# The job of the second layer's norms, moved one step later in the repeated part of a two-layer kernel

## The chip, the cores and the metric

The kernel runs on one core of one Trainium2 chip. The metric is device time in microseconds (us) of one execution. The kernel before takes 874.63 us (median of three runs, 871.47 to 875.64). Engines are called by the profile's names: PE (matrix products), DVE (vector), ACT (activations), POOL, and SP, which only issues transfers.

## The reference, cut to what matters

Two transformer layers work on x of shape (8, 512, 128): eight sequences of 512 tokens, width 128, 16 heads.

```
xn = layernorm(x)
x  = x + attention0(xn) + ffn0(xn)     # differential attention: two maps of 16 heads with 4 numbers each
xn = layernorm(x)
x  = x + attention1(xn) + ffn1(xn)     # rotated q and k, one map of 16 heads with 8 numbers each
```

Each attention is softmax(scale * q k^T) v per head. The feed-forward part of the second layer is three products (128 to 512 to 512 to 128) with weights of +1 and -1, and a relu after the first and the second.

The softmax is computed with a fixed shift in place of the row's maximum. That is allowed where a bound on the scores holds: for the second layer, the product of the largest norm of a q row and of a k row. The norms are what this case is about: two small products add up the squares of q and of k per head, and a chain of small vector operations makes a flag of them. If the flag says that the bound fails, an exact maximum is computed instead, and that branch is not taken with these inputs.

## The kernel before, in words

**Units and steps.** The attention work is 24 units in a fixed order. A(b) and B(b) are the two maps of the first layer for sequence b, C(b) is the second layer. A unit has 16 steps. In each step PE makes the scores of four heads against 128 keys (`scores`, L845, four products of 128x512 into the pairs of banks `ps_s`), ACT takes the exponential of them in two instructions (L707, two banks each), and PE multiplies the probabilities of the step before the last with the values (`pv`, L863, four products that add into one bank, `ps_pv`). So step s of a unit has on PE: scores(s), pv(s-2), and then the jobs of the step.

**Jobs.** Everything else (projections, feed-forward, norms, rotations) is put into steps by tables written out by hand: FIRST, LOOP and LAST (L75, L103, L120). LOOP holds one body of three units, A(b), B(b), C(b-1), and is written out for b = 2, 3, 4, 5. PE, DVE and ACT each walk the same table, and each runs its own part of every entry in the order of the table; each engine's queue runs in order. POOL and SP have no part in the entries spoken of here.

**One bank for all jobs.** The products of all jobs go to a single bank, `ps_misc`. Before a job's first product PE waits until the job before it has been read out of that bank (`PLAN.before`, L743). Who reads is in TAKER (L60): DVE for v1 and qk_norm1, ACT for ff0.

**The jobs around the change**, all in unit A(b), for sequence b-1 of the second layer:

- v1 (step 9): 32 products of 128x128 (L728), then DVE copies the bank to the values (L1167).
- take (step 9): no product. DVE waits for pv of step 7 and transposes `ps_pv` into `pv_sb` (L1308). PE's pv of step 8, the first of the next pair of head groups, waits for it (L869), as it starts anew in that bank.
- qk_norm1: two bf16 products of 32x512 (L779), then DVE reduces the bank to one number a row (L1170), which frees the bank, and six small operations make the flag (L1172 to L1183).
- ff0 with block 3 (step 10): two products (L732, L733), then ACT's relu (L657) into `ff_out`, and DVE splits that in two parts (L1104, L1106).
- project1 (step 11): 32 products (L728), DVE adds them to x.
- exact1 (step 12): PE and DVE read the flag (L813, L1242), and DVE sets the shift.

```
                if PLAN.before[item] is not None:
                    e, n = PLAN.before[item]
                    pe.wait_ge(TAKEN[e], n)
...
                pe.wait_ge(exps_made, 2 * S + 2)
                if s % 8 == 0:
                    wait(pe, pv_taken, 2 * U.u + s // 8)
```

Of the kernel before, what the change touches and what calls it, by code (L numbers as in the profile page):

```python
# [60 lines left out]
             qk_norm1="dve", w_t="dve", quant_t="dve", quant_mm="dve",  # L61
# [41 lines left out]
LOOP = [  # L103
    {0: [("ff0", -1, 0)], 1: [("take", -2, "C", 1), ("ff0", -1, 1)], 2: [("regroup", -2, "C", 1)], 3: [("q1", -1)],
     4: [("rope", -1, "q", 0), ("ff0", -1, 2)], 5: [("out_t1", -2), ("rope", -1, "q", 1)], 6: [("k1", -1)],
     7: [("rope", -1, "k", 0), ("rope", -1, "k", 1)], 9: [("v1", -1), ("take", 0, "A", 0), ("qk_norm1", -1)], 10: [("ff0", -1, 3)],
     11: [("regroup", 0, "A", 0), ("project1", -2)], 12: [("exact1", -1)], 13: [("ff1", -1, 0), ("ff1_b", -1, 0), ("norm0", 1, 0)],
     14: [("ff1", -1, 1), ("norm0", 1, 1)], 15: [("ff1_b", -1, 1), ("norm0", 1, 2)]},
    {0: [("ff1", -1, 2), ("norm0", 1, 3)], 1: [("take", 0, "A", 1), ("norm0", 1, 4), ("ff1_b", -1, 2)],
# [1371 lines left out]
```

## Time and profile before

| | us |
|---|---|
| median of three runs | 874.63 |
| the profiled execution | 872.51 |
| its span, first to last instruction | 870.7 |
| PE busy | 808.3 (93%) |
| ACT busy | 765.2 (88%) |
| DVE busy | 545.4 (63%) |
| POOL busy | 36.0 (4%) |

The span leaves 1.8 us of the execution's own time around it. PE and ACT pass work back and forth in every step. The profile's mean of PE's granted clock over the span is 0.98 of full speed. Busy shares are means over units of different kinds; the stretch of the change lies in the A units, and the rows below are of that stretch.

### The profile page before, as it was taken

What the parts mean: (1) busy time and instruction counts of PE and PEld (TensorE: products, weight loads), DVE (VectorE), ACT (ScalarE), POOL (GpSimd) and SP (SyncE); (2) the same over time, 40 slices, a digit from 0 to 9 for tenths busy, and PEclk for the clock granted to TensorE, in tenths of its full rate; (3) what the DMA queues carried; (4) which work ended last, traced back from release to release, by engine and by line L of the source; (5) the groups of instructions that cost most, each with busy time, mean ns of one, the idle gap of its engine ahead of it and who ended that gap; (6) DMA issues with size and microseconds to landing.
All of it is one profiled execution on the core that took longest, in us unless ns stands there. A gap on an engine that the chain in (4) does not pass through costs nothing.

```text
span 870.7 us, 17841 instructions
## 1 busy us (share of the span) xinstructions
PE 808.3 (93%) x6767; PEld 287.7 (33%) x6767; DVE 545.4 (63%) x1205; ACT 765.2 (88%) x856; POOL 36.0 (4%) x57
## 2 busy tenths in 40 slices
PE   6688898999999989999999999999998999999995
PEld 4122222342333323333233323333242323333342
DVE  6667478676774666746775567756677476476321
ACT  3679997889889998999889998999988999889984
POOL 5000000000000000000000000000000000000000
PEclk9889998999999999999999999999999999999998
DMA  6807315630728015460527407281164704205100
GB/s 182 170 9 149 52 50 148 146 49 8 209 49 142 11 69 142 104 99 1 148 62 142 59 1 209 50 138 16 49 162 100 102 17 133 52 1 167 43 13 13
DMA packets 41618, 75.52 MB, mean 87 GB/s; under 512 B 5872, under 2 KB 7024, under 8 KB 41520
## 3 DMA queue, kind: packets, MB, share of 16 engines
q1 hardware_dynamic: 39612, 68.45, 36.1%
q0 software_dynamic: 1824, 5.70, 2.1%
q8 instruction: 57, 0.93, 0.5%
q14 instruction: 33, 0.27, 0.1%
q10 hardware_dynamic: 92, 0.16, 0.1%
HBM read 36.84 MB, written 35.65 MB: 83 GB/s over the span
## 4 chain that ended last, share of the span: by engine, by line
PE 72%; ACT 11%; DVE 9%; issue 5%; DMA 1%; DVEq 0%; SPq 0%; ACTq 0%; POOL 0%; POOLq 0%
PE ps_pv L877 31%; PE ps_s L858 20%; ACT probs L707 11%; PE ps_misc L728 7%; PE ps_misc L732 7%; PE ps_misc L733 5%; PE ps_misc L721 2%; DMA q_ab<-shift 1%; DVE pv_sb L1308 1%; DVE v_aug L1167 1%; DVE tmp L1159 0%; DVE h_lo L1106 0%; DVE tmp L1158 0%; PE ps_misc L779 0%; ACT ff_out L657 0%
## 5 line engine op out<-in xcount | busy, mean ns | idle before, releaser
L707 ACT ACTIVATE probs<-ps_s 128x1024 f32<-128x1024 f32 x768 | 726.5, 1046 | 61.8 <-PE ps_s L858 60.5
L877 PE MATMUL ps_pv<-probs,v_aug 128*32 128x512 f32 x3072 | 413.5, 610 | 10.2 <-ACT probs L707 5.8
L858 PE MATMUL ps_s<-q_ab,k_ab 18*128 18x512 f32 (+1 forms) x1088 | 143.5, 500 | 28.8 <-ACT probs L707 20.3
L858 PEld LDWEIGHTS ps_s<-q_ab,k_ab 18*128 18x128 f32 (+1 forms) x1088 | 54.7, 184 | 197.7 <-ACT probs L707 153.7
L877 PEld LDWEIGHTS ps_pv<-probs,v_aug 128*32 128x32 f32 x3072 | 61.9, 108 | 118.5 <-issue 81.2
L732 PE MATMUL ps_misc<-h_hi,k_w 128*128 128x512 f32 x192 | 85.7, 446 | 2.7 <-DVE v_aug L1167 1.2
L858 PE MATMUL ps_s<-q_c,k_c 34*128 34x512 f32 x448 | 84.8, 453 | 0.0
L1104 DVE CAST h_hi<-ff_out 128x512 fp32r<-128x512 f32 x64 | 27.4, 428 | 89.0 <-ACT ff_out L657 87.5
L1308 DVE STREAM_TRANSPOSE pv_sb<-ps_pv 128x512 f32<-128x512 f32 x48 | 34.4, 717 | 70.8 <-PE ps_pv L877 67.5
L733 PE MATMUL ps_misc<-h_lo,k_w 128*128 128x512 f32 x192 | 75.9, 395 | 0.0
L732 PEld LDWEIGHTS ps_misc<-h_hi,k_w 128*128 128x128 f32 x192 | 35.9, 187 | 88.4 <-issue 48.8
L858 PEld LDWEIGHTS ps_s<-q_c,k_c 34*128 34x128 f32 x448 | 36.1, 184 | 74.7 <-ACT probs L707 60.2
L657 ACT ACTIVATE ff_out<-ps_misc 128x512 f32<-128x512 f32 x64 | 39.1, 610 | 17.9 <-PE ps_misc L733 13.8
L1106 DVE TENSOR_TENSOR h_lo<-ff_out,h_hi 128x512 fp32r<-128x512 f32 x64 | 44.3, 692 | 2.2
L733 PEld LDWEIGHTS ps_misc<-h_lo,k_w 128*128 128x128 f32 x192 | 36.1, 188 | 4.3
L1191 DVE TENSOR_TENSOR x_all<-ps_misc,x_all 128x512 f32<-128x512 f32 x24 | 16.6, 692 | 26.3 <-PE ps_misc L721 12.8
L728 PE MATMUL ps_misc<-xn_t,w_qk 128*32 128x512 f32 x248 | 32.3, 592 | 0.0
L1167 DVE COPY v_aug<-ps_misc 128x512 f32<-128x512 f32 x14 | 9.7, 692 | 27.5 <-PE ps_misc L728 27.1
L615 POOL CAST h_hi<-xn_t 128x512 fp32r<-128x512 f32 x8 | 4.9, 608 | 502.9 <-DVE xn_t L1135 502.9
L1320 DVE TENSOR_TENSOR heads<-pv_sb,recip 128x256 f32<-128x256 f32 x48 | 20.4, 425 | 1.7
L728 PE MATMUL ps_misc<-wp,quant_t 128*32 128x128 f32 x512 | 17.8, 282 | 2.7 <-DVE quant_t L1327 2.7
L728 PEld LDWEIGHTS ps_misc<-wp,quant_t 128*32 128x32 f32 x512 | 15.2, 113 | 12.8 <-issue 11.3
(164 smaller groups left out, 563.1 us busy)
## 6 DMA issues: line engine op xcount, KB each, us to landing
parts_dram<-qk_parts SPq DMA_DIRECT2D x32, 512.0 KB, 3.7
parts_dram<-qk_parts SPq DMA_DIRECT2D x62, 256.0 KB, 4.1
q_ab<-parts_dram SPq DMA_DIRECT2D x60, 128.0 KB, 4.6
k_ab<-parts_dram SPq DMA_DIRECT2D x60, 128.0 KB, 5.9
q_c<-parts_dram SPq DMA_DIRECT2D x14, 512.0 KB, 7.5
k_c<-parts_dram SPq DMA_DIRECT2D x14, 512.0 KB, 8.8
out_dram<-x_all POOLq DMA_DIRECT2D x8, 256.0 KB, 6.8
x_all<-in_L_attn_x_dram POOLq DMA_DIRECT2D x7, 256.0 KB, 6.1
```

The lines of the kernel that those rows point to most:

```text
L657: nc.scalar.activation(ff_out[:], ps_misc[:], ACT.Relu).then_inc(job_taken_act, 1)
L707: nc.scalar.activation(probs[:, U.slot(s), 2 * half:2 * half + 2], ps_s[:, 2 * pair:2 * pair + 2], ACT.Exp, scale=SCALE[U.layer]).then_inc ...
L728: ins = nc.tensor.matmul(ps[c, :], w[:, c], x, start=True, stop=True)
L732: nc.tensor.matmul(ps, w, hi, start=start, stop=False)
L733: return nc.tensor.matmul(ps, w, lo, start=False, stop=stop)
L858: ins = nc.tensor.matmul(ps_s[:, bank, :], k[row:row + n, slot, c * P:(c + 1) * P], q[row:row + n, slot, :], start=True, stop=True)
L877: ins = nc.tensor.matmul(ps_pv[32 * j:32 * j + 32, :], v_aug[:, U.v, c, a:a + 32], probs[:, U.slot(s), j, :], start=c == 0 and not odd, st ...
L1104: nc.vector.tensor_copy(hi, ff_out[:]).then_inc(ff_split, 1)
L1106: nc.vector.tensor_tensor(lo, ff_out[:], hi.bitcast(F32), ALU.subtract).then_inc(ff_split, 1)
L1167: taken(nc.vector.tensor_copy(own_values(unit("C" if layer else "A", b).v), ps.rearrange("p (t h e) -> p t h e", t=T, h=H)))
L1308: nc.vector.transpose(pv_sb[:], ps_pv[:]).then_inc(pv_taken, 1)
L1320: nc.vector.tensor_tensor(dst, v[:, :, :, 0:HD], rows(recip[:], HD), ALU.mult).then_inc(regroup_ops, 1)
```

## The change

In LOOP, the entry of qk_norm1 moves from the end of step 9 of unit A to the head of step 10, in front of the ff0 entry. Nothing else is changed: the order of the jobs in the bank `ps_misc` and the order of DVE's and ACT's work stay the same.

```diff
-     7: [("rope", -1, "k", 0), ("rope", -1, "k", 1)], 9: [("v1", -1), ("take", 0, "A", 0), ("qk_norm1", -1)], 10: [("ff0", -1, 3)],
+     7: [("rope", -1, "k", 0), ("rope", -1, "k", 1)], 9: [("v1", -1), ("take", 0, "A", 0)], 10: [("qk_norm1", -1), ("ff0", -1, 3)],
```

On PE the order was scores(9), pv(7), v1, qk_norm1, scores(10), pv(8), ff0. It is now scores(9), pv(7), v1, scores(10), pv(8), qk_norm1, ff0. FIRST and LAST, which have qk_norm1 for the sequences 0, 5, 6 and 7, are as before.

## Rows read from the trace of the kernel before

**Rows 1.** The page: busy time by engine, and the chain that ended last
```profile
PE 808.3 (93%) x6767; PEld 287.7 (33%) x6767; DVE 545.4 (63%) x1205; ACT 765.2 (88%) x856; POOL 36.0 (4%) x57
PE 72%; ACT 11%; DVE 9%; issue 5%; DMA 1%; DVEq 0%; SPq 0%; ACTq 0%; POOL 0%; POOLq 0%
```
**Rows 2.** Chain of waits in the second body: start, length, what
```profile
325.89 0.70 DVE v_aug L1167
327.03 0.44 PE ps_s L858 x4
```
**Rows 3.** Timeline of PE, same stretch: start, length, what, [idle before, releaser]
```profile
324.76 1.06 PE L728 MATMUL ps_misc<-w_v,xn_t 128*32 128x128 f32 x32
326.64 0.39 PE L779 MATMUL ps_misc<-qk_sq,head_sel 128*32 128x512 bf16 x2 [0.81 <-DVE v_aug L1167]
326.96 0.51 PE L858 MATMUL ps_s<-q_ab,k_ab 18*128 18x512 f32 x4
327.55 1.06 PE L877 MATMUL ps_pv<-probs,v_aug 128*32 128x512 f32 x8
328.55 0.50 PE L732 MATMUL ps_misc<-h_hi,k_w 128*128 128x512 f32 x1
```
**Rows 4.** Timeline of DVE, same stretch
```profile
325.89 0.69 DVE L1167 COPY v_aug<-ps_misc 128x512 f32<-128x512 f32 x1 [0.79 <-PE ps_misc L728]
326.69 0.72 DVE L1308 STREAM_TRANSPOSE pv_sb<-ps_pv 128x512 f32<-128x512 f32 x1
327.51 0.68 DVE L1170 TENSOR_REDUCE norm_max<-ps_misc 64x1 f32<-64x512 f32 x1
329.20 0.14 DVE L1183 CAST flags<-flag_f 1x1 int32<-1x1 f32 x1
```
**Rows 5.** Timeline of ACT, same stretch
```profile
327.56 1.94 ACT L707 ACTIVATE probs<-ps_s 128x1024 f32<-128x1024 f32 x2 [1.41 <-PE ps_s L858]
```
**Rows 6.** Timeline of PE, first and last of the four bodies
```profile
224.36 0.39 PE L779 MATMUL ps_misc<-qk_sq,head_sel 128*32 128x512 bf16 x2 [0.81 <-DVE v_aug L1167]
531.03 0.39 PE L779 MATMUL ps_misc<-qk_sq,head_sel 128*32 128x512 bf16 x2 [0.81 <-DVE v_aug L1167]
```
**Rows 7.** Timeline of PE and DVE behind the loop, jobs in steps of their own
```profile
633.30 1.06 PE L728 MATMUL ps_misc<-w_v,xn_t 128*32 128x128 f32 x32
634.29 0.50 PE L858 MATMUL ps_s<-q_ab,k_ab 18*128 18x512 f32 x4
795.14 1.06 PE L877 MATMUL ps_pv<-probs,v_aug 128*32 128x512 f32 x8
796.02 0.39 PE L779 MATMUL ps_misc<-qk_sq,head_sel 128*32 128x512 bf16 x2
796.45 0.68 DVE L1170 TENSOR_REDUCE norm_max<-ps_misc 64x1 f32<-64x512 f32 x1 [0.16 <-PE ps_misc L779]
```
**Rows 8.** Timeline of DVE and PE ahead of the loop, PE waiting for the reduction
```profile
133.96 0.68 DVE L1170 TENSOR_REDUCE norm_max<-ps_misc 64x1 f32<-64x512 f32 x1
134.69 1.08 PE L728 MATMUL ps_misc<-w_v,xn_t 128*32 128x128 f32 x32
```
**Rows 9.** Timeline of PE around two falls of its clock
```profile
140.05 0.50 PE L732 MATMUL ps_misc<-h_hi,k_w 128*128 128x512 f32 x1 [1.16 <-DVE v_aug L1167]
141.47 0.50 PE L732 MATMUL ps_misc<-h_hi,k_w 128*128 128x512 f32 x1 [0.69 <-ACT ff_out L657]
671.19 1.77 PE L877 MATMUL ps_pv<-probs,v_aug 128*32 128x512 f32 x8 [1.93 <-DVE pv_sb L1308]
676.06 0.51 PE L858 MATMUL ps_s<-q_ab,k_ab 18*128 18x512 f32 x4
```
**Rows 10.** Busy time by stretch; the number behind POOL's is PE's granted clock
```profile
140.00:150.00 10.00, 9.03 (x44) 2.77 (x48) 6.99 (x21) 5.62 (x8) 0.00 (x0) 0.66 0.60 126
670.00:680.00 10.00, 8.64 (x84) 2.96 (x84) 4.04 (x8) 6.65 (x8) 0.00 (x0) 0.83 0.97 187
320.00:330.00 10.00, 8.60 (x95) 3.03 (x96) 7.90 (x18) 8.40 (x11) 0.00 (x0) 1.00 0.74 247
```

## The prediction

> **What bounds the kernel now.** I read four views, in this order. The page first: PE is busy for 93% of the span and ACT for 88%, and the chain that ended last lies on PE for 72% and on DVE for only 9% [rows 1]. So a wait matters where it holds PE up; DVE's own load does not. Second, the chain of waits in the stretch of the change, for the question whether the moved job is on it. It is: DVE's copy of v stands in the chain with 0.70 us, and the norm products and the scores behind it are fed from it [rows 2]. Third, the timelines of PE, DVE and ACT side by side. On PE the reader is to see one gap of 0.81 us, in front of the norm products, while DVE copies v out of the shared bank [rows 3]; on ACT a gap of 1.41 us, as the scores of step 10 stand behind those products [rows 5]. The same gap of 0.81 us stands in each of the four bodies of the loop, of which the first and the last are shown [rows 6]. That is what the change removes. Fourth, the stretches with PE's granted clock, for what gaps have done to it.
>
> **What goes.** PE no longer waits for the copy of v before step 10. Where v and the next scores follow without a job between them, the scores start 634.29 - 633.30 = 0.99 us after the second part of v's products [rows 7]. Here that is 324.76 + 0.99 = 325.75, against 326.96 before [rows 3]: 1.21 us earlier. They last 0.51 us, to 326.26.
>
> **What is late next.** Behind these scores stands pv(8), and it waits for something else: for DVE's transposition of the same bank (take). DVE does that behind the copy of v. The copy can't start earlier than now, since v's products don't; it runs from 325.89 for 0.69, and the transposition from 326.69 for 0.72, so to 327.41 [rows 4]. PE's pv(8) starts at 327.55, 0.14 later [rows 3], and 0.59 behind its scores where the chain gives scores 0.44 [rows 2]. So it is the transposition that already sets pv(8) before the change, and pv(8) stays at 327.55. All of the 1.21 us is given back there, as a gap of 327.55 - 326.26 = 1.29 us on PE.
>
> **What is added.** Now the norm products stand behind pv(8), and ff0 behind them in the same bank, with the reduction by DVE between the two. Step by step, from pv(8)'s start:
>
> - pv to norm products: 796.02 - 795.14 = 0.88 us [rows 7], so 328.43.
> - norm products to reduction: 796.45 - 796.02 = 0.43, with DVE idle before it [rows 7], so 328.86. Here DVE is free from 327.41.
> - the reduction: 0.68 [rows 7], so to 329.54.
> - its end to PE's next product: 134.69 - (133.96 + 0.68) = 0.05 [rows 8], so ff0 starts at 329.59.
>
> Before the change ff0 started at 328.55 [rows 3], since the reduction (327.51 to 328.19 [rows 4]) was hidden behind scores and pv of step 10. That cover is gone, and with it PE gains a second gap, from the end of the norm products, 328.43 + 0.39 = 328.82, to 329.59: 0.77 us. Loss: 329.59 - 328.55 = 1.04 us in each body.
>
> Queued behind ff0 are on PE the scores of step 11, and on ACT its relu, with the exponentials of step 11 behind that. ACT gets the scores of step 10 some 1.2 us earlier but then stands before the relu, so its head start doesn't last. All of PE, ACT and DVE go on 1.04 us later. I find nothing with a fixed time that would take this up: DMA has 1% of the chain [rows 1]. The six small operations behind the reduction end 329.34 - 328.19 = 1.15 us after it [rows 4], so at 330.69; the flag's reader is two steps on, behind ff0, a step's scores and pv and 32 products of project1, which alone take more than that. No transfer is moved, no POOL or SP instruction either. Sum of the waits: 4 x 1.04 = 4.2 us.
>
> **What the gaps do to the clock.** The trace has two places where PE's clock fell from 2.4 to 1.2 GHz within work like this. At 140.05 and 141.47 PE had gaps of 1.16 and 0.69 us, 1.85 in all between 138.89 and 141.47; at 671.19 it had one of 1.93 [rows 9]. In the first stretch the granted clock averages 0.66 over 10 us, which is 0.34 x 10 / 0.5 = 6.8 us at the lower level; in the second 0.83, so 3.4 us [rows 10]. The single gap of 0.81 of now left it at 1.00 [rows 10]. The change makes gaps of 1.29 and 0.77 us, 2.06 in all, from 326.26 to 329.59. That looks like the rows where the clock fell, not like the one where it held; but the two gaps stand further apart than those, so I don't expect it each time. Price of one fall: from 671.19 to 676.06 PE did pv, scores, pv and v in 4.87 us [rows 9]. At full speed these are 1.00 [rows 3], 0.44 [rows 2], 0.88 and 0.99 [rows 7], in sum 3.31. So 1.6 us for the shorter fall; for the longer I take twice that, 3.1. The bounds over four bodies are 0 and 4 x 3.1 = 12.4 us; I take one fall of the short kind in the four, 1.6, as the nearest row is a single gap of nearly this sum and the two gaps here are spread more.
>
> The Trainium skill's page "TensorE: Matmul & The Clock Gate", section "Why this matters for your kernels", says that the clock drops mid-kernel for one idle gap far longer than either of these. By that rule no body would meet a fall, and the sum would be the waits alone. The trace does not agree with it: at 140 no single gap was over 1.16 us, and the clock fell all the same [rows 9, 10].
>
> **Sum.** 4.2 + 1.6 = 5.8 us. The profiled execution took 872.51 (span 870.7 and 1.8 around it), so it would take 878.3. It lies 2.1 under the median of the runs, 874.63; the median is what a set of new runs is compared with, so I predict 874.63 + 5.8 = 880.4 us.
>
> **Rivals.**
>
> 1. *The waits alone, the clock holds.* For it: the gap of 0.81 did nothing to the clock, and the new gaps are separated by 1.3 us of products. Against it: the pair at 140. Time: 874.63 + 4.2 = 878.8.
> 2. *The clock falls in three or four bodies.* For it: 2.06 us of gaps are more than either row. Time: 4.2 + 3 x 1.6 = 9.0, so 883.6; with the longer kind up to 4.2 + 4 x 3.1 = 16.6, 891.
> 3. *Faster: pv(8) doesn't wait for the transposition.* Place: PE's wait in step 10. If it passed at once, pv(8) would start at 325.75 + 0.44 = 326.19, the norm products at 327.07, the reduction at 327.51 (the transposition ends at 327.41, so DVE is just free), and ff0 at 327.51 + 0.68 + 0.05 = 328.24 against 328.55: 0.31 us gained in each body, 1.2 in all, 873.4. It decides by whether pv(8) starts before 328.55 - 2.04 = 326.51, as the four steps above take 2.04 us from there to ff0. Against it: pv(8) follows the transposition's end by 0.14 now.
> 4. *Taken up later.* The 1.04 us of a body could vanish in slack downstream: 874.6. For it speaks only that the chain has 5% "issue" time that the profile doesn't explain [rows 1].
>
> **How the numbers follow.** A difference of about 0.5% (4.4 us) is what a measurement here can tell from none. Chances: the forecast (waits and one or two falls) 0.42; rival 1, 0.30; rival 2, 0.16; rival 3, 0.05; rival 4, 0.07. Forecast and rival 2 lie over 4.4 us. Rival 1 lies at 4.2, just inside, so I split it, 0.12 over and 0.18 within. Rivals 3 and 4 are within, except for 0.03 which I leave for a gain of over 0.5% that no row shows. So slower 0.70, same 0.27, faster 0.03. The range leaves out rival 3 and the far half of rival 2: 876.0 to 886.0; its lower end holds rival 1 in a set of runs as fast as the profiled one (872.51 + 4.2 = 876.7).
>
> **What would show it.** In the changed kernel's timeline of PE: scores of step 10 right behind v, in each of four bodies; a gap of about 1.3 us before pv(8), released by DVE's transposition of ps_pv; norm products 0.88 behind that pv; a gap of about 0.8 us before ff0, released by the reduction. On ACT: the exponentials of step 10 some 1.2 us earlier, and a gap of about 2 us before the relu. The distance from v's products to ff0 grows by 1.04 us. Stretches of the granted clock around the four bodies show whether it fell, and how often. The prediction is wrong if pv(8) starts earlier after v than now, if ff0 keeps its distance to v, or if the bodies (now (531.03 - 224.36) / 3 = 102.2 us apart [rows 6]) don't grow by 1 us or more.

## The result, and the profile after

The changed kernel is slower. In a first set of seven runs its median is 883.44 us (877.44 to 884.08) against 872.83 for the kernel before; the ratio is 1.0102, with a 95% interval of 1.0072 to 1.0132, so 8.9 us by the ratio (10.6 between the two medians). In a second set on another occasion (experiment after_again) it is 878.08 against 872.49, ratio 1.0071, 1.0046 to 1.0097, so 6.2 us. The forecast was 5.8 us: 4.2 of waits and 1.6 of one fall of PE's clock. The waits came out within 0.02 us a body. What comes on top of them is more than the 1.6 (4.7 and 2.0 us by the two ratios) and varies from one execution to the next; part of it is the clock.

The profiled execution took 877.44 us, the shortest of the first set. Its span, from the page:

```profile
span 875.6 us, 17841 instructions
PE 807.9 (92%) x6767; PEld 287.8 (33%) x6767; DVE 545.4 (62%) x1205; ACT 765.5 (87%) x856; POOL 36.0 (4%) x57
```

The busy times are those of before [rows 1] within 0.4 us, so the 4.9 us that the span has grown is no added work. The timeline of PE in the second body (start, length, what, idle before and who ended it), to be read against [rows 3]:

```profile
326.81 1.06 PE L728 MATMUL ps_misc<-w_v,xn_t 128*32 128x128 f32 x32
327.79 0.51 PE L858 MATMUL ps_s<-q_ab,k_ab 18*128 18x512 f32 x4
329.59 1.06 PE L877 MATMUL ps_pv<-probs,v_aug 128*32 128x512 f32 x8 [1.29 <-DVE pv_sb L1308]
330.45 0.41 PE L779 MATMUL ps_misc<-qk_sq,head_sel 128*32 128x512 bf16 x2
331.63 0.50 PE L732 MATMUL ps_misc<-h_hi,k_w 128*128 128x512 f32 x1 [0.78 <-DVE norm_max L1170]
```

The reader is to see two gaps where there was one of 0.81 us, each with the releaser that the prediction named. From v to ff0 it is now 331.63 - 326.81 = 4.82 us; before it was 328.55 - 324.76 = 3.79 [rows 3]. That is 1.03 us more. The timeline of DVE, against [rows 4]:

```profile
327.93 0.69 DVE L1167 COPY v_aug<-ps_misc 128x512 f32<-128x512 f32 x1 [0.78 <-PE ps_misc L728]
328.73 0.72 DVE L1308 STREAM_TRANSPOSE pv_sb<-ps_pv 128x512 f32<-128x512 f32 x1
330.90 0.68 DVE L1170 TENSOR_REDUCE norm_max<-ps_misc 64x1 f32<-64x512 f32 x1 [1.45 <-PE ps_misc L779]
```

DVE stands 1.45 us between its second and its third operation. Before, it had the norm products ready for it there. And of ACT, against [rows 5]:

```profile
328.40 1.94 ACT L707 ACTIVATE probs<-ps_s 128x1024 f32<-128x1024 f32 x2 [0.21 <-PE ps_s L858]
332.40 0.60 ACT L657 ACTIVATE ff_out<-ps_misc 128x512 f32<-128x512 f32 x1 [2.07 <-PE ps_misc L733]
```

ACT starts step 10's exponentials 1.59 us after the start of v's products instead of 2.80, and gives it back in front of the relu. The chain of waits has both of DVE's operations on it now:

```profile
327.93 0.70 DVE v_aug L1167
328.73 0.73 DVE pv_sb L1308
329.59 1.06 PE ps_pv L877 x8
330.90 0.69 DVE norm_max L1170
```

Last, the stretches by the four bodies; the number behind POOL's is PE's granted clock, 1.00 everywhere in the same four stretches before:

```profile
220.00:240.00 20.00, 17.42 (x168) 7.16 (x164) 11.37 (x25) 14.40 (x17) 0.61 (x1) 0.91 0.72 188
325.00:345.00 20.00, 17.42 (x176) 7.61 (x172) 12.83 (x28) 15.71 (x18) 0.58 (x1) 1.00 0.72 188
430.00:450.00 20.00, 17.49 (x173) 7.58 (x166) 12.02 (x27) 15.44 (x19) 0.56 (x1) 1.00 0.69 175
535.00:555.00 20.00, 17.96 (x148) 7.41 (x148) 12.71 (x35) 15.31 (x18) 0.56 (x1) 1.00 0.64 156
```

The clock fell once, in the first body: 0.09 x 20 / 0.5 = 3.6 us at 1.2 GHz. What that costs can be read from the distance between the reductions (L1170) of successive bodies, which start like this:

```profile
225.98 0.68 DVE L1170 TENSOR_REDUCE norm_max<-ps_misc 64x1 f32<-64x512 f32 x1 [1.45 <-PE ps_misc L779]
330.90 0.68 DVE L1170 TENSOR_REDUCE norm_max<-ps_misc 64x1 f32<-64x512 f32 x1 [1.45 <-PE ps_misc L779]
434.02 0.68 DVE L1170 TENSOR_REDUCE norm_max<-ps_misc 64x1 f32<-64x512 f32 x1 [1.45 <-PE ps_misc L779]
537.39 0.68 DVE L1170 TENSOR_REDUCE norm_max<-ps_misc 64x1 f32<-64x512 f32 x1 [1.45 <-PE ps_misc L779]
```

| | body 1 to 2 | 2 to 3 | 3 to 4 |
|---|---|---|---|
| before | 102.28 | 102.06 | 102.33 |
| after | 104.92 | 103.12 | 103.37 |
| difference | 2.64 | 1.06 | 1.04 |

The second and third differences are the waits alone; the first has the fall as well, 2.64 - 1.05 = 1.6 us. So this execution is the forecast nearly term by term: 4 x 1.04 + 1.6 = 5.8. From the last reduction ahead of the loop to the first one behind it the time grew from 502.11 to 507.71 us, by 5.6. The whole execution grew by 4.9 (877.44 - 872.51); the difference lies ahead of and behind the loop.

### The profile page after: what moved, and what is told of

It is laid out like the page before. It is cut to its first block, busy times and chain, and to the rows that moved or that the text cites. A ratio compares the mean times of both kernels' runs of the same rounds, so it can differ in the third digit from the quotient of the medians.

```text
span 875.6 us, 17841 instructions
## 1 busy us (share of the span) xinstructions
PE 807.9 (92%) x6767; PEld 287.8 (33%) x6767; DVE 545.4 (62%) x1205; ACT 765.5 (87%) x856; POOL 36.0 (4%) x57
## 4 chain that ended last, share of the span: by engine, by line
PE 71%; ACT 11%; DVE 10%; issue 5%; DMA 1%; DVEq 0%; SPq 0%; ACTq 0%; POOL 0%; POOLq 0%
PE ps_pv L877 31%; PE ps_s L858 19%; ACT probs L707 11%; PE ps_misc L728 7%; PE ps_misc L732 7%; PE ps_misc L733 5%; PE ps_misc L721 2%; DMA q_ab<-shift 1%; DVE pv_sb L1308 1%; DVE v_aug L1167 1%; DVE norm_max L1170 0%; DVE h_lo L1106 0%; ACT ff_out L657 0%; DVE tmp L1159 0%; DVE tmp L1089 0%
## 5 line engine op out<-in xcount | busy, mean ns | idle before, releaser
L1308 DVE STREAM_TRANSPOSE pv_sb<-ps_pv 128x512 f32<-128x512 f32 x48 | 34.4, 717 | 70.9 <-PE ps_pv L877 67.5
```

Source lines behind the costliest of these rows:

```text
L1308: nc.vector.transpose(pv_sb[:], ps_pv[:]).then_inc(pv_taken, 1)
```

## The experiments

**Fill the gaps.** If what exceeds 4.2 us is the clock, it must go when PE has something to do in the gaps, though the waits stay. Of the edits only the lines and entries that differ are shown; "..." marks what is left out between them.

```diff
+            def fill(S, n):
+
+                pe.wait_ge(exps_made, 2 * S)
+                for _ in range(n):
+                    nc.tensor.transpose(ps_s[:, 2 * ((2 * S + 2) % 3), 0:P], ident[:], ident[:])
...
                     scores(U, s)
+                    if U.kind == "A" and U.b in range(2, 6) and s == 10:
+                        fill(U.first_step + s, 7)
...
+                            if S % STEPS == 10:
+                                fill(S, 4)
```

> The changed kernel with both of PE's new gaps filled: in step 10 of the four bodies PE does 7 transposes of the identity after the scores and 4 after the norm products, into a bank of ps_s that is free there and is written anew by the next scores. The waits stay where they are, as the fill is about as long as the gaps (1.0 of 1.29 us and 0.6 of 0.77 us). Theory (the time over the 4.2 us of waits is lost to falls of PE's clock): the clock no longer falls in the bodies, and the time is 872.8 + 4.2 = 877.0, with runs close to each other (within 2 us beside those of the kernel before). Rival (the waits cost more than the trace shows, or something else is lost): the time stays at 881 to 884 as in the changed kernel.

Measured: 877.39 us against 874.04 before in the same set, ratio 1.0048 (1.0029 to 1.0067), 4.2 us. The timeline of PE in its first body:

```profile
227.65 0.98 PE L885 MATMUL ps_s<-ident 128*128 128x128 f32 x7
229.00 1.06 PE L877 MATMUL ps_pv<-probs,v_aug 128*32 128x512 f32 x8 [0.36 <-DVE pv_sb L1319]
230.20 0.66 PE L885 MATMUL ps_s<-ident 128*128 128x128 f32 x4
231.04 0.50 PE L732 MATMUL ps_misc<-h_hi,k_w 128*128 128x512 f32 x1 [0.19 <-DVE norm_max L1181]
```

The work starts where it did (229.00 - 227.20 = 1.80 us from scores to pv, as 329.59 - 327.79 = 1.80 above), and the granted clock is 1.00 in all four bodies. The time is that of the waits alone, within an interval of 2.5 to 5.9 us. That interval lies below that of the first set of the changed kernel (1.0072 to 1.0132) and overlaps with that of the second (1.0046 to 1.0097), so the timed runs alone don't settle what the fill gives back. One part of the expectation missed: the runs were not within 2 us of each other (876.18 to 882.66), so the bodies aren't the only place where executions differ. The profiled execution shows it: it took 880.70 us with no fall in the bodies, and it is 2.9 us behind the kernel before already at the last reduction ahead of the loop (136.87 against 133.96).

With only the second gap filled (the edit is against the one above):

```diff
-                        fill(U.first_step + s, 7)
+                        fill(U.first_step + s, 0)
```

> The changed kernel with only the second gap (before ff0, 0.77 us) filled, by 4 transposes of the identity; the gap of 1.29 us before pv of step 8 stays. Theory (it takes both gaps for the clock to fall, as single ones of 1.29 us in the spread version's profile were followed by no fall): 877 to 878, as with both filled. Rival (the gap of 1.29 us is enough by itself in some executions): 879 to 883, with falls in the bodies of the profile.

878.13 us against 872.49, ratio 1.0057 (1.0032 to 1.0082), 5.0 us. In its profile no body had a fall, though each had the gap of 1.29 us. That agrees with the theory that it takes both gaps, but one profile of four bodies can't exclude a rare fall. The time says nothing either way: the changed kernel with nothing filled took 878.08 us in the same set, so on those runs the fill gained nothing that can be measured.

**The same kernel again**, for more profiles of the changed kernel with their times.

> The changed kernel once more, unaltered, for a second profile beside its time. Its first profiled execution took 877.44 us with one fall of the clock in the four bodies, while most of its other runs took 882 to 884. Theory: those have two to four falls of some 1.6 us or more. So this profile, if it lies at 881 or more, shows at least two stretches at the lower level within the four bodies, and each body without one is 103.2 us from the next; if it lies under 879 it shows one at most. Rival (the waits themselves last longer in the slow executions): the gaps before pv of step 8 and before ff0 differ from 1.29 and 0.77 us, with no more falls.

> The changed kernel once more, one look, for a third profile beside its time. Expected as in the second: the time over 876.4 to 877 is 1.6 us or more for each fall of the clock in the four bodies, give or take the 1 to 2 us that the falls ahead of and behind the loop differ by between executions.

> The changed kernel once more, one look. The three profiles so far had one fall in the four bodies each, at 877.4 to 879.6 us; its slowest executions, at 883 to 884, were not seen yet. If this one takes over 881 us, the theory wants two falls or more in the bodies; if under 880, none or one.

> The changed kernel once more, one look, expected as the fourth: over 881 us two falls or more in the bodies, under 880 none or one.

| profile | time | falls in the bodies | distances of the bodies |
|---|---|---|---|
| first | 877.44 | body 1 | 104.92, 103.12, 103.37 |
| after_again | 877.47 | body 1 | 104.88, 103.09, 103.34 |
| after_look3 | 879.63 | body 3 | 103.40, 103.08, 104.92 |
| after_look4 | 879.55 | body 3 | 103.36, 103.08, 104.93 |
| after_look5 | 883.67 | bodies 1 and 4 | 104.88, 103.11, 103.36 |

The gaps are 1.28 to 1.29 and 0.78 us in all twenty bodies; so the waits are the same whatever an execution takes, and the rival falls. Six of the twenty bodies have a fall, and in all six it shows first behind the second gap: ff0's first product takes 0.58 to 0.80 us there instead of 0.50. The twenty are not independent draws. The three executions with a fall in body 1 have their last reduction ahead of the loop at 133.5 to 134.0 us; the two with one in body 3 have it at 135.8, and are alike to within 0.1 us at every reduction. That also accounts for most of their 879.6 us: they have one short fall, as the first profile has, and are 2.2 us behind it before the loop begins. The one of 883.67 us has two, as expected, the second of the long kind (a stretch and a line of PE in after_look5):

```profile
535.00:550.00 15.00, 12.81 (x100) 5.50 (x100) 6.32 (x16) 8.79 (x11) 0.56 (x1) 0.77 0.87 215
693.87 0.51 PE L858 MATMUL ps_s<-q_ab,k_ab 18*128 18x512 f32 x4 [3.35 <-DMA q_ab<-shift]
```

0.23 x 15 / 0.5 = 6.9 us at 1.2 GHz. From the fourth body's reduction to the next one, behind the loop, it is 106.65 us, against 103.83 in the first profile: 2.8 us for a long fall. But its span is 881.9 - 875.6 = 6.3 us over the first profile's, and 3.4 of these lie outside the bodies, between 644 and 739 (95.04 against 91.61 from one reduction to the next), around the second line above: a wait of 3.35 us for the transfer of the shift, where the first profile has 0.70.

**The tail.** In both kernels the clock as a rule falls around 671 to 677, behind a gap of 1.93 us [rows 9]. In after_look5 it didn't, and the long wait came in its place. To see whether the one makes the other, the kernel before had that gap filled:

```diff
+                    if (U.kind, U.b, s) == ("B", 6, 10):
+                        fill(U.first_step + s, 10)
```

> The kernel before (norm products in their old place), in which PE fills its gap of 1.93 us in step 10 of unit B(6), behind the loop, with 10 transposes of the identity (1.5 us) after the scores, into a bank of ps_s that is free there. In the kernel before that gap is followed by a fall of the clock, and PE then waits only 0.49 us for the transfer of the shift at the start of unit A(7). In the changed kernel's slow profile (883.67 us) the clock did not fall there, PE waited 3.35 us for that transfer instead, and the clock fell behind that wait, for 6.8 us. Theory (a tail of the time of both kernels comes from there): with the gap filled the clock doesn't fall at 671, PE waits 2 to 3.5 us for the transfer, the clock falls behind it, and the time is 2 to 3.5 us longer than the kernel before, 874.5 to 876. Rival (the transfer's lateness in the slow profile has another cause): no fall, the wait grows by at most 1.5 us, and the time is that of the kernel before or up to 1 us less.

876.27 us against 874.46, ratio 1.0031 (1.0013 to 1.0049): 2.7 us slower. PE, and the granted clock behind POOL's number:

```profile
670.83 1.31 PE L896 MATMUL ps_s<-ident 128*128 128x128 f32 x10 [0.41 <-ACT probs L707]
672.35 1.06 PE L877 MATMUL ps_pv<-probs,v_aug 128*32 128x512 f32 x8 [0.21 <-DVE pv_sb L1316]
687.55 0.64 PE L858 MATMUL ps_s<-q_ab,k_ab 18*128 18x512 f32 x4 [4.15 <-DMA q_ab<-shift]
```
```profile
670.00:680.00 10.00, 9.21 (x102) 4.08 (x106) 5.16 (x9) 8.22 (x9) 0.00 (x0) 1.00 0.84 174
685.00:695.00 10.00, 7.07 (x40) 2.26 (x40) 1.68 (x4) 5.18 (x6) 0.68 (x1) 0.83 0.77 98
```

Without the fall PE waited 4.15 us for the transfer instead of 0.49, more than the 2 to 3.5 expected, and the clock fell behind that wait. PE's early arrival is the smaller part of it. With the two profiles laid over each other at the first reduction behind the loop (636.07 and 637.23), PE comes to the wait 1.6 us earlier, and the transfer lands 2.1 us later. The chain of waits has the transfer itself, first in the kernel before, then with the gap filled:

```profile
679.60 4.62 DMA q_ab<-shift
679.96 7.51 DMA q_ab<-shift
```

It goes the same way in the other profiles: 4.84 and 4.70 us in the first profile and after_again, where the clock fell ahead of it, 6.49 in after_look5, where it didn't. An earlier PE also frees its operands earlier, and the next unit's loads are then issued 3.3 us behind the transfer (682.56 - 679.28) instead of 4.0 (682.97 - 678.93); it is 3.3 in after_look5 and 4.0 in the first profile, too. That these loads slow it down is likely and was not tested. From that first reduction to the next one it is 94.96 us against 91.36 before, 3.6 more, so here the fall ahead of the wait cost nothing, and doing away with it did. How often either kernel runs without that fall is not known: one of five profiles of the changed kernel did, and the one profile of the kernel before has it.

**A longer second gap.**

```diff
+                    if b in range(1, 5):
+                        nc.vector.tensor_reduce(stat[0:64, 1, 60:61], ps[0:64, :], AX.X, ALU.max)
```

> The changed kernel, in which DVE reduces the bank of the norm products twice in each of the four bodies (first to a number nobody reads), so that PE's second gap is longer by one reduction: 1.29 and then 0.77 + 0.71 = 1.48 us, 2.77 in all. The waits then cost 4 x (1.04 + 0.71) = 7.0 us over the kernel before. Theory (the clock falls when enough of PE's gaps lie close together, and the changed kernel's 2.06 us do it only sometimes): with 2.77 us it falls in nearly all bodies, 4 x 1.6 or more on top, 13.4 us or more slower than before: 886 or more, with three or four falls in the bodies of the profile. Rival (falls come by chance with any gap of this kind, about one in four bodies): 7.0 + 1.6 = 8.6, 881.

886.75 us against 872.31, ratio 1.0169 (1.0148 to 1.0190), 14.7 us. The time is the theory's (886 or more), the profile is not (three or four falls). PE's gaps in its second body, and three of its stretches:

```profile
329.21 1.06 PE L877 MATMUL ps_pv<-probs,v_aug 128*32 128x512 f32 x8 [1.29 <-DVE pv_sb L1310]
331.86 0.79 PE L732 MATMUL ps_misc<-h_hi,k_w 128*128 128x512 f32 x1 [1.37 <-DVE norm_max L1172]
```
```profile
220.00:240.00 20.00, 16.84 (x170) 7.22 (x167) 12.85 (x28) 15.25 (x18) 0.61 (x1) 1.00 0.73 190
325.00:345.00 20.00, 17.05 (x152) 7.58 (x152) 10.28 (x23) 13.23 (x16) 0.58 (x1) 0.83 0.70 180
535.00:555.00 20.00, 16.82 (x171) 7.40 (x168) 12.85 (x28) 15.26 (x18) 0.56 (x1) 1.00 0.72 185
```

With 2.66 us of gaps in each body the clock fell in one of four, here for 0.17 x 20 / 0.5 = 6.8 us. The two reductions overlap in part, so the gap grew by 0.6 and not 0.71 us, and the waits are 4 x 1.65 = 6.6. This profile, the fastest run of the set (884.90), has no fall behind the gap of 1.93 us and the tail's wait instead (3.55 us; the transfer took 6.90). It adds up: 6.6 of waits, some 2.8 for the long fall and 3.9 in the tail (95.23 us from one reduction to the next against 91.36) are 13.3, with 12.4 measured over the profile of before. So the time met the theory's figure largely by the tail, for which neither theory nor rival had a term. The theory that more gap makes a fall nearly certain is not borne out in this one profile; the rival's count is right and its 881 us is not. The other three runs took up to 3.2 us more, and no trace shows where.

**Take first.** The first gap is DVE's order: the transposition waits behind the copy of v.

```diff
-9: [("v1", -1), ("take", 0, "A", 0)], 10: [("qk_norm1", -1), ("ff0", -1, 3)],
+9: [("take", 0, "A", 0), ("v1", -1)], 10: [("qk_norm1", -1), ("ff0", -1, 3)],
```

> The changed kernel with one more edit: in step 9 the entry of take stands ahead of that of v1, so that DVE transposes ps_pv before it copies v. Theory (of the waits): pv of step 7 has ended before v's products do, so the transposition is done some 1.5 us earlier than in the changed kernel and pv of step 8 follows the scores with no gap. Only the second gap (before ff0, 0.7 to 0.8 us) is left, and ff0 starts about 0.3 us earlier after v than in the kernel before: 4 x 0.3 = 1.2 us faster than before (872.8), so 871.6; the clock holds, as in the kernel before. Rival (it is the place of the norm products behind pv, or the head start of ACT, that costs): the time stays near that of the changed kernel, 877 to 884.

872.74 us against 874.04, ratio 0.9995 (0.9975 to 1.0014): the loss is gone. One of its twelve runs took 1775.38 us, twice the time; it is not in the ratio, and no trace shows what happened in it. PE in the first body:

```profile
223.93 0.51 PE L858 MATMUL ps_s<-q_ab,k_ab 18*128 18x512 f32 x4
224.36 1.07 PE L877 MATMUL ps_pv<-probs,v_aug 128*32 128x512 f32 x8
226.41 0.50 PE L732 MATMUL ps_misc<-h_hi,k_w 128*128 128x512 f32 x1 [0.78 <-DVE norm_max L1170]
```

pv follows its scores by 0.43 us, and the bodies are (531.63 - 225.67) / 3 = 101.99 us apart against 102.22 before: 0.23 us gained in each where 0.3 was expected, which the timed runs can't tell from nothing. No body of this profile has a fall. The norm products' new place costs only together with DVE's order. The same order with the norm products in their old place:

```diff
-9: [("v1", -1), ("take", 0, "A", 0), ("qk_norm1", -1)], 10: [("ff0", -1, 3)],
+9: [("take", 0, "A", 0), ("v1", -1), ("qk_norm1", -1)], 10: [("ff0", -1, 3)],
```

> The kernel before with take ahead of v1 in step 9, and the norm products left in step 9. Theory: the gap of 0.81 us for the copy of v stays; pv of step 8, which now follows the transposition by 0.14 us, follows its scores and is 0.15 us earlier in each body: 0.6 us faster than before in all, 872.2, which the measurement can hardly tell from none. Rival (the transposition is what costs in either kernel): over 2 us faster than before.

872.50 us against 874.04, ratio 0.9987 (0.9972 to 1.0002), bodies 102.29 apart. The rival falls. The expected 0.15 us isn't there either: the gap for the copy of v grew from 0.81 us to between 0.91 and 1.27 in the four bodies, as the copy now starts behind the transposition.

**A version that beats both** lets a step's scores and pv stand between any two jobs.

```diff
-9: [("v1", -1), ("take", 0, "A", 0)], 10: [("qk_norm1", -1), ("ff0", -1, 3)],
-11: [("regroup", 0, "A", 0), ("project1", -2)], 12: [("exact1", -1)],
+9: [("take", 0, "A", 0), ("v1", -1)], 10: [("qk_norm1", -1)],
+11: [("regroup", 0, "A", 0), ("ff0", -1, 3)], 12: [("exact1", -1), ("project1", -2)],
```

> A version that should beat both: take ahead of v1 in step 9, the norm products in step 10 alone, ff0 with block 3 in step 11 and project1 in step 12, so that a step's scores and pv stand between any two jobs of the shared bank. Theory: PE has neither the gap of 0.81 us nor the 0.15 us before pv of step 8 nor a new one; 4 x 0.96 = 3.8 us faster than before, 869.0, if ACT is no later than PE there. Rival (ACT sets the pace once PE's gap is gone): ACT's own gap of 1.41 us per body shrinks only in part and the gain is under 2 us, 871 to 873.

872.61 us against 874.04, ratio 0.9998 (0.9982 to 1.0014): no gain, and for neither theory's reason. The gap had moved to a place I hadn't worked out, DVE setting the shift ahead of project1's addition:

```profile
230.38 0.48 DVE L1270 MEMSET shift<- 16x512 f32 x1 [0.95 <-DVE h_lo L1106]
231.52 0.69 DVE L1191 TENSOR_TENSOR x_all<-ps_misc,x_all 128x512 f32<-128x512 f32 x1
```
```profile
232.27 0.50 PE L732 MATMUL ps_misc<-h_hi,k_w 128*128 128x512 f32 x1 [1.28 <-DVE x_all L1191]
```

With exact1 a step later (the edit is against the version just shown):

```diff
-12: [("exact1", -1), ("project1", -2)], 13: [("ff1", -1, 0),
+12: [("project1", -2)], 13: [("exact1", -1), ("ff1", -1, 0),
```

> As the spread version (take ahead of v1, norm products in step 10, ff0 in step 11, project1 in step 12), but exact1, which reads the flag and sets the shift, moves from step 12 to step 13. In the spread version DVE did the two memsets of the shift ahead of project1's addition and PE stood 1.28 us before ff1. Theory: that gap goes, as the addition now comes first, and no other takes its place: over 3 us faster than before (872.8 to 874.0), 869 to 870.5. Rival (ACT sets the pace once PE's gap is gone, or the gap moves on to another of PE's waits): under 1.5 us faster.

868.60 us against 872.49, ratio 0.9949 (0.9932 to 0.9965), 4.4 us faster than before and 9.5 faster than the changed kernel in the same set (878.08). PE has no gap of over 0.6 us in the bodies; they are (528.75 - 226.16) / 3 = 100.86 us apart, 1.36 less than before. That is the theory's outcome, a little better than its 869 to 870.5. The runs lie within 1.8 us (867.58 to 869.36).

## Why the prediction was right, point by point

- *The gap of 0.81 us goes, scores 0.99 behind v.* Right: 0.98.
- *The transposition holds pv(8), a gap of 1.29 us.* Right: 1.29, released by L1308. Taking it ahead of v removed the gap (take first).
- *pv to norm products 0.88, to the reduction 0.43, 0.68, and 0.05 to ff0.* 0.86, 0.45, 0.68, 0.05. All four come from stretches of other sequences, and held.
- *1.04 us in each body, 4.2 in all, nothing takes it up.* Right: 1.03 from v to ff0, 1.04 and 1.06 between bodies, and 4.2 us with both gaps filled.
- *ACT's head start of 1.2 us is lost in front of the relu.* Right: 1.21 us earlier, a gap of 2.07.
- *One short fall of 1.6 us among the four bodies.* The price is right (1.6 for a short one; 2.8 for a long one, where I had 3.1), and so is the likeliest number: four of five profiles have one. That it was one and not two was a choice and not worked out, so that much is luck. So is part of how near 880.4 came: the base of 874.63 was 1.8 above the 872.83 of seven runs, and the two sets of the changed kernel lie 3.0 above the forecast and 2.3 below it. The mean is 1.2 falls, and the term is short for the first set: by the ratios the share over the waits is 8.9 - 4.2 = 4.7 us there and 2.0 in the second. The term "one fall of the short kind" was mis-sized for the executions of 882 us and more. The one that was looked into (after_look5) has a second, long fall, and the tail behind the loop, 3.4 us, which the prediction had no term for. The mean clock of the first set's five longest runs (0.968 to 0.977, against 0.98 in the shortest) fits with more falls, but runs of the kernel before have such values too, and there is no trace of those five; why that set lies 5 us above the second stays open.
- *Two gaps of 2.06 us look like the rows where the clock fell.* Right in kind. That it comes in some bodies and not in others with the same gaps was the right doubt; the longer gap of the experiment with two reductions brought one fall in the four bodies of its profile.
- *The Trainium skill's rule.* The page "TensorE: Matmul & The Clock Gate", in "Why this matters for your kernels", names only one long gap as the cause of a drop mid-kernel. Six falls in twenty bodies with no gap over 1.29 us show otherwise. Another section of that page, "A second HAM failure mode: psum-queue depth-cycling", tells of a kernel whose clock swings as PE idles briefly and often between groups of products while it cycles through banks; these traces agree with it as to the short idle times; there is only one bank for the jobs here.

## What to carry to other kernels

A job moved behind a step's main work saves its wait only if nothing else is waiting there: look up what each of the next instructions waits for, since a wait hidden behind the one you remove takes its place. With one bank for all jobs, as here, two jobs in one step showed the reader's time between them wherever nothing filled it (0.78 us and more); put a step's own work between any two, and check the second engine's order in the step that they are moved to. And two gaps of about a microsecond close together on PE can cost more than their length: here 1.6 or 2.8 us more, in some bodies.

## What the runs showed of the hardware that I had not expected

The same two gaps (1.29 and 0.78 us) let the clock fall in six of twenty bodies, not the same ones in each execution, for 3.4 or 6.8 us, at a price of 1.6 or 2.8 us each. With eleven transposes of data nobody reads in those gaps it stayed at 2.4 GHz in all four bodies of the one profile; as fourteen of twenty bodies have no fall without them either, that alone is weak evidence. And a fall that stood ahead of a wait for a transfer was worth keeping: without it the kernel before was 2.7 us slower (1.1 to 4.3), as the transfer then took 7.51 us in place of 4.62.
